# First attention: the causal mask of the exponents by a select on POOL in place of a matmul, the values four units behind, a ring of eight

## What is computed

```python
x = x + 0.5 * _L0_ffn_ref(_layernorm(x, axis=-1), ...)
x = x + _L0_attn_ref(_layernorm(x, axis=-1), L0_attn_Wqkv, L0_attn_Wo, ...)
x = x + 0.5 * _L0_ffn_ref(_layernorm(x, axis=-1), ...)
...
# in _L0_attn_ref, b batches, 16 heads:
scores = einsum('bhqd,bhkd->bhqk', q_rot, k_rot) / sqrt(dh) + decay_bias
scores = jnp.where(causal[None, None], scores, jnp.float32(-jnp.inf))
attn = jax.nn.softmax(scores, axis=-1)
out = jnp.einsum('bhqk,bhkd->bhqd', attn, v)
```

## Time and profile before

| what | us |
|---|---|
| median of three runs | 1912.04 (1908.57 to 1916.41) |
| the profiled execution, its own time | 1891.98 |
| its span | 1890.2 |
| first attention, first to last mask matmul of L1531 | 309.3 to 677.9 of the span |

### The profile page before, as it was taken

How to read it: one execution, slowest core, us unless ns; L and a number is a source line. 1 busy time by engine, 2 the same in 40 slices (tenths; PEclk the granted TensorE clock), 3 DMA queues, 4 the chain that set the end, 5 groups by cost and what they waited for, 6 DMA issues and landing times. The chain is left out here.

```text
span 1890.2 us, 34789 instructions
## 1 busy us (share of the span) xinstructions
PE 1355.6 (72%) x10592; PEld 873.5 (46%) x10592; DVE 1184.6 (63%) x4256; ACT 718.7 (38%) x1340; POOL 941.9 (50%) x1276
## 2 busy tenths in 40 slices
PE   2359929988889859963369916777777777876990
PEld 2249914444444428962258803333333333335880
DVE  6622256888888632228845547877787787745555
ACT  1112215666666512210023313544444544532330
POOL 5745534455555224547747745444544544433770
PEclk9999957999999959985579956866776676767995
DMA  9312217553000002222158710000000000004874
GB/s 292 97 51 72 68 45 155 114 119 70 22 20 13 13 17 63 72 79 77 58 150 243 226 56 12 7 18 14 16 15 13 17 6 7 13 18 144 238 231 141
DMA packets 105373, 146.40 MB, mean 77 GB/s; under 512 B 14192, under 2 KB 84336, under 8 KB 105264
## 3 DMA queue, kind: packets, MB, share of 16 engines
q1 hardware_dynamic: 85824, 107.13, 21.4%
q0 software_dynamic: 17408, 35.82, 5.6%
q10 hardware_dynamic: 2032, 2.10, 0.4%
HBM read 80.59 MB, written 64.40 MB: 77 GB/s over the span
## 5 line engine op out<-in xcount | busy, mean ns | idle before, releaser
L1370 ACT ACTIVATE a_PT<-a_psE 128x512 f32<-128x512 f32 (+1 forms) x512 | 276.0, 545 | 300.7 <-PE a_psE L1539 297.8
L1074 DVE TENSOR_REDUCE a_mx<-a_psS 128x2 f32<-128x512 f32 (+1 forms) x512 | 308.4, 615 | 18.9 <-PE a_psS L1502 17.7
L1502 PE MATMUL a_psS<-a_KT,a_QT 54*128 54x256 bf16 (+1 forms) x1024 | 203.9, 302 | 76.4 <-DVE a_mx L1074 62.5
L1539 PE MATMUL a_psE<-a_QM,a_KT 56*128 56x256 bf16 (+1 forms) x1024 | 208.6, 306 | 1.5 <-issue 0.8
L1563 PE MATMUL a_psV<-a_PT,a_vx 128*32 128x256 f32 (+1 forms) x2048 | 185.9, 442 | 0.0
L1975 POOL DMA_INDIRECT slots_y<-e_y,e_ids x160 | 155.7, 973 | 46.6 <-issue 24.4
L1897 PE MATMUL e_psH<-e_rowsT,e_w 128*128 128x256 f32 x640 | 160.3, 395 | 5.1 <-DMA e_w<-in_pack 3.7
L1502 PEld LDWEIGHTS a_psS<-a_KT,a_QT 54*128 54x128 bf16 x1024 | 61.6, 100 | 206.5 <-issue 108.1
L1811 POOL DMA_INDIRECT slots_y<-e_y,e_ids x128 | 124.6, 974 | 48.2 <-POOL e_ids L1809 28.7
L1775 ACT ACTIVATE e_hT<-e_psH 128x1024 f32<-128x1024 f32 x64 | 65.5, 1024 | 179.5 <-PE e_psH L1748 179.5
L1897 PEld LDWEIGHTS e_psH<-e_rowsT,e_w 128*128 128x128 f32 x640 | 118.5, 195 | 23.5 <-issue 5.1
(11 more groups left out here) (337 smaller groups left out, 3258.4 us busy)
## 6 DMA issues: line engine op xcount, KB each, us to landing
e_w<-in_pack SPq DMA_DIRECT2D x80, 450.0 KB
slots_x<-tail SPq DMA_DIRECT2D x8, 2193.0 KB, 13.5
e_rows<-slots_x SPq DMA_DIRECT2D x80, 129.0 KB, 2.9
e_rows<-spans_x SPq DMA_DIRECT2D x64, 129.0 KB
a_got<-slots_y SPq DMA_DIRECT2D x32, 256.0 KB, 2.7
t_got<-slots_y SPq DMA_DIRECT2D x32, 256.0 KB, 2.8
slots_y<-e_y,e_ids POOLq DMA_INDIRECT x288, 2.2
spans_x<-tail SPq DMA_DIRECT2D x4, 1032.0 KB, 17.1
```

The lines of the kernel that those rows point to most:

```text
L1074: nc.vector.tensor_reduce(mx[u][:, t, 4 * g + r:4 * g + r + 3:2], psS[c % 2][:, :, 0:cols], AX, ALU.max).then_inc(s_max, 1)
L1370: nc.scalar.activation(PT[:, c % 4, :, q0:SEQ], psE[c % 2][:, :, q0:SEQ], ACT.Exp).then_inc(s_e, 1)
L1502: ins = nc.tensor.matmul(psS[c % 2][:, hh, 0:cols], QT[u][64 * r:64 * r + MAXR, k, t * P:(t + 1) * P], KT[u][64 * r:64 * r + MAXR, k, 0:co ...
L1539: ins = nc.tensor.matmul(psE[c % 2][:, hh, q0:SEQ], KT[u][64 * r:64 * r + MAXR + 2, k, kt * P:(kt + 1) * P], QM[64 * r:64 * r + MAXR + 2, ...
```

## The change

The mask matmul of `e_open` goes, and `e` starts its own accumulation. In its place POOL sets the masked exponents to zero after ACT has written them: `cut(b, c)` waits for the exponent of unit c, adds one to a semaphore (`s_seen`), and runs one `affine_select` over the 128 x 2 x 128 block of the ring on which the diagonal lies, 16 times in a step. `unit_v` waits for the cut (`s_cut`), not for the exponent. The values run four units behind in place of two (`LAG`), the ring has eight places in place of four (`RING`), and units 12 to 15 stand at the end of the step. POOL's step is written anew (`step_with_cuts`): the 16 cuts stand between its other work, the rotation is moved ahead of the scatters and split in two parts, and the four scatters are issued one by one. ACT's `weighted_out` stands one unit later. The second attention has the same instructions as before.

```diff
+            def cut(b, c):
+                g, r, kt = unit_c(c)
+                pool.wait_ge(s_e, UNITS * b + c + 1)
+                pool.sem_inc(s_seen, 1)
+                block_of = PT[:, c % RING, :, kt * P:(kt + 1) * P]
+                nc.gpsimd.affine_select(out=block_of, in_=block_of, pattern=[[0, 2], [1, P]], compare_op=ALU.is_ge,
+                                        fill=0.0, base=0, channel_multiplier=-1).then_inc(s_cut, 1)
...
+            def step_with_cuts(s, u):
...
+                cuts(0, 2)
+                    left_of_a(s + 1, v)
+                cuts(2, 5)
+                    left_of_b(s + 1, v)
+                cuts(5, 8)
+                    norm.pool_rstd(pool, s + 3, v)
+                cuts(8, 10)
+                do(halves, 0)
+                cuts(10, 11)
+                do(halves, 1)
+                cuts(11, 12)
+                do(pieces, 0)
+                cuts(12, 13)
+                do(pieces, 1)
+                cuts(13, 14)
+                do(pieces, 2)
+                    route.norm.pool_rstd(pool, s - 2, u)
+                cuts(14, 15)
+                do(pieces, 3)
+                cuts(15, 16)
+                chain.restart()
...
-                wait(act, s_V, UNITS * b + c - 3)
-                nc.scalar.activation(PT[:, c % 4, :, q0:SEQ], psE[c % 2][:, :, q0:SEQ], ACT.Exp).then_inc(s_e, 1)
+                wait(act, s_V, UNITS * b + c - (RING - 1))
+                nc.scalar.activation(PT[:, c % RING, :, q0:SEQ], psE[c % 2][:, :, q0:SEQ], ACT.Exp).then_inc(s_e, 1)
...
-                if causal:
-                    nc.tensor.matmul(psE[c % 2][:, :, kt * P:(kt + 1) * P], identb[:, :],
-                                     masks[:, 1, :].unsqueeze(1).to_broadcast([P, 2, P]), start=True, stop=False,
-                                     skip_group_check=True)
...
-                pe.wait_ge(s_e, UNITS * b + c + 1)
+                pe.wait_ge(s_cut if causal else s_e, UNITS * b + c + 1)
...
-                    if has(s - 1) and n >= 2 and n % 2 == 0:
-                        unit_v(s - 1, v, n - 2)
-                        unit_v(s - 1, v, n - 1)
+                    if has(s - 1) and n >= LAG and n % 2 == 0:
+                        unit_v(s - 1, v, n - LAG)
+                        unit_v(s - 1, v, n - LAG + 1)
...
-                    unit_v(s - 1, v, UNITS - 2)
-                    unit_v(s - 1, v, UNITS - 1)
+                    for c in range(UNITS - LAG, UNITS):
+                        unit_v(s - 1, v, c)
```

More of the change, by code:

```diff
@@ L542, in pool_scatter, with pool_rows @@
     def pool_scatter(self, pool, chain, b, w):
+        self.pool_rows(pool, chain, b, w)
+        for k in range(TPB * TOPK):
+            self.scatter_one(pool, w, k)
+    def pool_rows(self, pool, chain, b, w):
         if self.clean and is_first(b):
@@ L546, in pool_scatter, with scatter_one, scatter_pieces, first @@
         chain(self.nc.gpsimd.tensor_tensor(self.rows[:, w, :], self.rows0[:, w, :], self.keep.no_rows[:, :], ALU.add))
-        for k in range(TPB * TOPK):
-            pool.indirect_dma_start(
-                self.slots, bass.IndirectOffsetOnAxis(ap=self.rows[:, w, k:k + 1].bitcast(U32), axis=0),
-                self.norm.out[:, w, k // TOPK, k % TOPK, :], None).then_inc(self.s_scat[w], 16)
+    def scatter_one(self, pool, w, k):
+        pool.indirect_dma_start(
+            self.slots, bass.IndirectOffsetOnAxis(ap=self.rows[:, w, k:k + 1].bitcast(U32), axis=0),
+            self.norm.out[:, w, k // TOPK, k % TOPK, :], None).then_inc(self.s_scat[w], 16)
+    def scatter_pieces(self, pool, chain, b, w):
+        def first():
+            self.pool_rows(pool, chain, b, w)
+            self.scatter_one(pool, w, 0)
+        def rest(k):
+            return lambda: self.scatter_one(pool, w, k)
+        return (first, *[rest(k) for k in range(1, TPB * TOPK)])
     def pool_end(self, pool):
@@ L994, in left_of_b, with cuts, do @@
                 nc.gpsimd.tensor_tensor(flat(left2), flat(left), both(u, 4), ALU.subtract).then_inc(s_l2, 1)
+            def cut(b, c):
[6 more added lines that the diff above has]
+            def step_with_cuts(s, u):
+                v = 1 - u
+                def cuts(lo, hi):
+                    for c in range(lo, hi):
+                        if has(s - 1):
+                            cut(s - 1, c)
+                halves = rotate(s + 2, u) if has(s + 2) else ()
+                pieces = route.scatter_pieces(pool, chain, s - 3, v) if has(s - 3) else ()
+                def do(which, n):
+                    for piece in which[n:n + 1]:
+                        piece()
+                cuts(0, 2)
+                if has(s + 1):
+                    left_of_a(s + 1, v)
+                cuts(2, 5)
+                if has(s + 1):
+                    left_of_b(s + 1, v)
+                cuts(5, 8)
+                if has(s + 3):
+                    norm.pool_rstd(pool, s + 3, v)
[9 more added lines that the diff above has]
+                do(pieces, 2)
+                if has(s - 2):
+                    route.norm.pool_rstd(pool, s - 2, u)
[3 more added lines that the diff above has]
+                chain.restart()
             def step(s, u):
                 v = 1 - u
-                if has(s + 1) and not causal:
+                if causal:
+                    step_with_cuts(s, u)
+                    return
+                if has(s + 1):
                     scale_heads(s + 1, v)
@@ L1001, in step @@
                     left_of_a(s + 1, v)
-                if has(s) and not causal:
+                if has(s):
                     output_bias(s)
@@ L1011, in step @@
                     route.norm.pool_rstd(pool, s - 2, u)
-                if has(s + 2) and causal:
-                    rotate(s + 2, u)
-                if has(s + 2) and not causal:
+                if has(s + 2):
                     refine(s + 2)
@@ L1405, in step @@
                 exps(9, 10)
-                if has(s - 1):
+                if has(s - 1) and not causal:
                     weighted_out(s - 1, v)
                 exps(10, 11)
+                if has(s - 1) and causal:
+                    weighted_out(s - 1, v)
                 if has(s + 2) and not causal:
@@ L1540, in e @@
                     psE[c % 2][:, hh, q0:SEQ], KT[u][64 * r:64 * r + MAXR + 2, k, kt * P:(kt + 1) * P],
[L1541 removed]
+                    QM[64 * r:64 * r + MAXR + 2, k, q0:SEQ], start=True, stop=True, skip_group_check=True)
                 if hh == 1:
```

34 lines of the change are left out of this document (20 added, 14 removed).

## The result

The changed kernel takes 1971.0 us (median of 4 runs, 1962.6 to 1976.6), against 1910.3 us (4 runs, 1882.4 to 1916.4) for the kernel before. The ratio is 1.040, with a 95% interval of 1.025 to 1.054: slower. The profiled execution took 1962.6 us.

The account below looks back on a forecast made before the run. PE's queue was taken to set the step, with DVE close behind. Eleven steps of 8.7 us more, three of 6 and -2 for the first two give 111 us; 1912 + 111 = 2023 us, range 1958 to 2080.

Parts of the forecast that it names:

- the late queue: POOL's last cut stands behind rotation and scatters, so PE's last values come 5 to 6 us late in each step.
- exponent 0 to exponent 9, at the lower clock: First part of a step: 9.5 us at full clock, plus 2.5 with half the stretch at the lower clock.
- exponent 9 to the last cut, POOL waiting for no other engine: POOL's remaining queue: rotation 4.3, row numbers and scatters 5.3, power 0.7, seven cuts 3.9 us; 14.2 in all.
- last cut to the next exponent 0: End of a step, POOL idle: 5.0 us, plus 1.2 at the lower clock for transposes, L408 and unit 0.
- step at the full clock: Length of a full first-attention step without the clock's fall: 9.5 + 10.4 + 3.9 + 5.0 = 28.8 us, 5.0 more than before.
- the stage: First attention: eleven steps of 8.7 us more, three of 6 and -2 for the first two, 111 us.
- The select: One cut on POOL: 0.45 us for the operation plus 0.10 for wait and semaphore, between bounds of 0.34 and 1.04.
- The clock: PE's new gap of 6 us puts the start of nearly each step at 0.50, adding 2.5 + 1.2 us.
- That is all that the change can give: 16 steps x 1.6 = 26 us: PE without 16 mask matmuls a step of 0.11 us: 1.8 us, of which 1.6 is gained after waits for DVE's maxima.
- Rotating earlier gives nothing: POOL's rotation moved ahead of the scatters brings no gain, as DVE reads its result in the next step.
- the rival in which POOL is in time: POOL's cuts come in time and the masks' 26 us are gained, 1886 us; chance 0.06.
- 1972: Rival total in us: queue late but clock stays full, 1912 + 60; chance 0.20.

Follow-up runs that it names:

- the fill in the gap: Changed kernel plus twenty matmuls of 512 columns that nobody reads, between PE's last groups of values: 2030.9 us, ratio 1.048.
- scatters last: Changed kernel with the four scatters behind the last cut of POOL's step and the power ahead of cut 14: 1979.8 us, ratio 1.022.
- deferred: Changed kernel with scatters one step later, between cuts 3 and 8, and the rotation behind the last cut: 1922.2 us, ratio 1.017.

## Why the prediction was right and where it was off

The direction was right, and so was the mechanism of the loss (the late queue); the range (1958 to 2080) held the time, and the time, 2023, was 52 us too high. Step by step:

| the prediction's step | predicted | measured |
|---|---|---|
| exponent 0 to exponent 9, at the lower clock | 12.0 us | 12.67 |
| exponent 9 to the last cut, POOL waiting for no other engine | 14.2 | 13.05 |
| last cut to the next exponent 0 | 6.2 | 5.81 |
| step | 32.5 | 31.5 here; full steps 28.6 to 32.6 |
| step at the full clock | 28.8 | 28.0 (28.8 with the fill in the gap, less its 0.8) |
| one select, wait included | 0.55 | 0.41, follow-on start after 0.37 |
| last cut behind exponent 15 | 5 to 6 (values late) | 6.05 |
| the stage | +111 | +92 |
| the rest of the kernel | 0 | -21 in that profile |

**The queue.** It is as forecast: the cuts stand in POOL's order behind rotation and scatters, POOL waits for no other engine from exponent 9 to the last cut, then none of its work is ready for 6 us. Doubling the selects (+52 us) and moving the scatters out of the way (-27 us) both bear it out by experiment.

**The select.** The term was mis-sized: 7 x 0.14 us a step, some 14 us over fourteen steps. The nearest row that I took was the right kind (one input, tensor-scalar), and the answer lies at the lower end of my bounds. The fixed cost that I gave the wait isn't paid when the queue runs full: the next operation starts 0.37 us after a select of 0.41. An estimate from the Trainium skill, GPSIMD Engine Reference, section "Performance pitfalls for Q7 kernels", had the operation at 0.37 to 0.58 us without a wait, and the row of 0.41 agrees with its unrolled figure.

**The clock.** It falls in the place that was named. It doesn't fall equally in each step (28.6 us at 0.92 twice, 32.6 at 0.76). Step by step, the eleven full steps grew by 82.8 us and not by 95, and the first two became 1.5 us shorter and not 3. The last two grew by 10.4 us; I had put in three of 6, and the third lies outside the 15 steps measured. By the rule of the Trainium skill, TensorE: Matmul & The Clock Gate, section "HAM oscillation", a wait that recurs starts each tile at the lower clock; the rows from 505 to 525 agree, the two steps at 0.92 only in part.

**Where it was wrong.** Two of its steps failed, and they didn't show in the total, since POOL's queue sets the step here. "That is all that the change can give: 16 steps x 1.6 = 26 us" was an upper bound that isn't reached at all: without its masks the kernel before is 0.65% slower. PE's work did fall by the predicted amount (1.66 us a step). But I took only 0.2 us of it as lost to waiting, and at the full clock PE waits for DVE for 1.4 us more. And the clock was put down to the new gap alone. With no late queue (scatters last, no mask at all, deferred) it is still 0.79 to 0.83 over the stage, and full steps are 25 to 30 us long. With no late queue the masks matter for it. In POOL's new order it is 0.93 over the stage with them and 0.79 without, though on two chips; in the old order, on one chip, the clock over the whole kernel falls from 0.815 to 0.797 (medians of 19 and 10 runs). So the rival in which POOL is in time would not have given 1886 us. By the ratios of the kernel without masks (1.007) and of the deferred one (1.017) on 1910.3 us I estimate 1924 to 1943. "Rotating earlier gives nothing" held for the time, but not for DVE: in the kernel without any mask its casts take up to 0.83 us beside the rotation, and L1080 and L1081 gain as much, from 0.58 and 0.64 us on the mean of the stage to 0.29 and 0.31 (L1157 and L1158 there).

**Slips in its sums.** Eleven steps of 5.0 us more are 55 and not 54 us. The last three steps use 2.1 us where the text has 2.4. And 1972 less the 14 x 1.4 us of a select of 0.35 us is 1952, not 1958. None of them moves the forecast by more than 6 us, and the measured time lies above either bound.

**The 52 us.** They are three parts. The stage grew by 92 and not by 111: 19 us. The rest of that profile was 21 us shorter (70.6 - 91.7), which is no effect of the change: 15 steps of the second attention took from 480 to 500 us in the profiles of kernels that are alike there. And I had set the median 20 us above the profiled time, where after it was 8.4: 12 us.

**What stays open.** Whether the clock follows PE's missing work or the waits that come in its place. The waits go the same way as the clock. Six matmuls leave 0.4 us ahead of L408 in most steps of the kernel before, at 1.00, and 1.2 to 1.3 us in the deferred one, at 0.92, which also waits 24.4 us for maxima against 10.3. Unfilled, the wait is 1.8 us in the kernel before (1.00 or 0.91), 2.0 to 2.3 without its masks (0.87) and 2.6 in the deferred kernel (0.83). No run changes the waits alone, without giving PE more work. Nor is it shown why the deferred kernel takes 27.3 us in each of its eleven full steps, where the kernel before without masks has steps of 23.4 and of 28.4. Single profiles differ by up to 27 us in this stage, so they don't settle the order of the kernels between 370 and 375 us; that is taken from the medians.

## What to carry to other kernels

Put the producer of the last thing that another engine waits for early in an in-order queue: count all that the queue still has behind the last common event, not its share of busy time, which was 53% here. Before you take work off the engine that sets the step, ask how far behind it the next engine is and what holds its clock, and take a second profile: a stage that is at 1.00 in one execution may stand at an edge. Where PE waits anyway, matmuls that nobody reads can be worth more than those that are saved.

## What the runs showed of the hardware that was not expected

- The same program has its first attention at a clock of 1.00 or of 0.91 in two executions (347.6 and 374.7 us), and 15 steps of the second attention, with equal instructions, took between 480 and 500 us in 13 profiles.
- Less work for PE, with longer waits for DVE in its place, made a kernel slower: 1.007 (1.002 to 1.011), at a clock of 0.797 against 0.815 over the whole kernel.
- DVE's cast of 128x256 from f32 to bf16 takes 0.83 us beside POOL's tensor-tensor operations and 0.28 without. Two operations of L343 take 0.59, 0.88 and 1.43 us in three kernels, with POOL's rotation beside them for 0.22, 0.54 and 1.35 us. That they contend is argued from their places in the timeline; the two were not measured apart.
- A select of 128x256 f32 on POOL takes 0.41 us, and a scatter still holds POOL's queue for 0.97 to 1.06 us beside it.
